# Graph attention on one core: gathers that leave out foreign edges, and 256-column fills on GpSimd

## The reference

```
q = (xn @ wq + bq).reshape(n, H, DH)            # H = 8 heads, DH = 32
k, v likewise; src, dst get one self edge for each node
scores = einsum('ehd,ehd->eh', q[dst], k[src]) * scale
ex = exp(scores - segment_max(scores, dst)[dst])
attn = ex / segment_sum(ex, dst)[dst]
agg = segment_sum(attn[:, :, None] * v[src], dst)
h = h + agg @ wo + bo ;  h = h + gelu(layernorm(h) @ w1 + b1) @ w2 + b2
```

## Time and profile before

| | us |
|---|---|
| median of 3 runs | 5238.9 (5233.25 to 5239.08) |
| profiled execution | 5237.06 |
| its span in the trace | 5235.3 |
| granted TensorE clock, mean | 0.899 of full speed |

### The profile page before, as it was taken

The page is one execution under the profiler, slowest core; times in us unless marked ns, Lnnn a source line. Parts: engine busy times, 40 slices in busy tenths (PEclk is TensorE's granted clock), DMA queues, the critical chain, the costliest instruction groups (busy, mean ns, idle before and its releaser), DMA issues. The chain is left out here.

```text
span 5235.3 us, 86953 instructions
## 1 busy us (share of the span) xinstructions
PE 3812.7 (73%) x17590; PEld 3000.8 (57%) x17591; DVE 3650.4 (70%) x9882; ACT 2132.3 (41%) x5069; POOL 3941.4 (75%) x4715
## 2 busy tenths in 40 slices
PE   1695777777777778888685777777777767777759
PEld 0344555555555567778443555555555557766646
DVE  3696888888888856666474888888888844444458
ACT  0113555555555523333113555555555523333322
POOL 2217888888888647777787888888888658888867
PEclk9898999999999989998896999899999978888879
DMA  3366666667666556666676766677666456666658
GB/s 112 118 201 199 201 199 199 197 197 201 198 196 199 144 129 140 139 130 134 117 156 176 203 197 199 197 196 202 199 198 197 134 128 127 125 123 126 132 142 238
DMA packets 664282, 882.62 MB, mean 169 GB/s; under 512 B 126257, under 2 KB 492269, under 8 KB 664013
## 3 DMA queue, kind: packets, MB, share of 16 engines
q0 software_dynamic: 261248, 529.64, 42.8%
q1 hardware_dynamic: 369907, 322.55, 20.8%
q10 hardware_dynamic: 32860, 28.05, 1.9%
HBM read 749.33 MB, written 130.59 MB: 168 GB/s over the span
## 5 line engine op out<-in xcount | busy, mean ns | idle before, releaser
L859 POOL DMA_INDIRECT kv<-kv_scratch,src_u x1760 | 1687.4, 959 | 364.3 <-POOL spacer L839 189.4
L1130 PE MATMUL sum_p<-msg,hot_s 128*128 128x273 f32 x3520 | 1091.6, 458 | 736.5 <-issue 499.5
L1318 POOL DMA_INDIRECT sum_scratch<-ysum,dest x700 | 1100.9, 1573 | 284.1 <-issue 153.5
L1130 PEld LDWEIGHTS sum_p<-msg,hot_s 128*128 128x128 f32 x3520 | 716.7, 215 | 1024.5 <-issue 697.5
L1118 PE MATMUL qe<-sums,hot_q 128*128 x3520 | 900.6, 401 | 74.5 <-ACT hot_q L890 48.8
L1118 PEld LDWEIGHTS qe<-sums,hot_q 128*128 128x128 f32 x3520 | 715.5, 206 | 216.9 <-issue 84.6
L996 DVE SCALAR_TENSOR_TENSOR sums<-sums,keep,sum_p 128x273 f32 x880 | 434.6, 494 | 436.7 <-PE sum_p L1130 326.5
L899 ACT ACTIVATE hot_s<-iota_f,ndrel_u 128x128 f32<-128x128 f32 x1760 | 559.4, 391 | 307.2 <-PE sum_p L1130 209.5
L970 DVE TENSOR_TENSOR prod<-qe,kv 128x1024 f32<-128x1024 f32 x440 | 535.9, 1218 | 67.5 <-DMA kv<-kv_scratch,src_u 66.4
L839 POOL MEMSET spacer<- 128x384 bf16 x1320 | 573.9, 435 | 0.9
L985 DVE TENSOR_TENSOR msg<-kv,turned 128x1024 f32<-128x1024 f32 x440 | 533.1, 1212 | 44.3 <-issue 34.6
(11 more groups left out here) (247 smaller groups left out, 5237.7 us busy)
## 6 DMA issues: line engine op xcount, KB each, us to landing
drow<-drel_scratch SPq DMA_DIRECT2D x220, 256.0 KB
ea<-in_edge_attr SPq DMA_DIRECT2D x100, 512.0 KB
srow<-in_src_rows SPq DMA_DIRECT2D x100, 512.0 KB
kv<-kv_scratch,src_u POOLq DMA_INDIRECT x1760
kv_scratch<-res SPq DMA_DIRECT2D x100, 256.0 KB
hin<-h_scratch SPq DMA_DIRECT2D x154, 128.0 KB
h_scratch<-res SPq DMA_DIRECT2D x150, 128.0 KB
masks<-mask_scratch SPq DMA_DIRECT2D x110, 128.2 KB
```

The source lines that it names most:

```text
L859: g.indirect_dma_start(out=kv[:, slot, :], out_offset=None, in_=KVd, in_offset=bass.IndirectOffsetOnAxis(ap=src_u[:, par, u:u + 1], axis=0 ...
L1130: ins = pe.matmul(sum_p[i][:, 0:XW], hot_s[:, q % 2, 2 * i + u, :], msg[:, q % 2, 2 * i + u, :], start=(u == 0), stop=(u == 1))
L1318: g.indirect_dma_start(out=sum_d[r], out_offset=bass.IndirectOffsetOnAxis(ap=dest[:, k, j:j + 1], axis=0), in_=ysum[:, k, j, :], in_offset ...
```

## The change

It has three parts. (1) The setup phase computes `later`, FAR = 8192 for units from number 48 on and else 0, and `skip`, which is `later` where an edge is not valid in its unit, and adds it to the source index. The first three periods (48 units) are left alone, so each ring slot is once filled in full. (2) The gather gets the bound NPA - 1 = 6911: an index above it is not fetched, and its row of `kv` keeps what it had. (3) The fills have 256 columns instead of 384.

```diff
+FAR = 1 << 13
+assert FAR >= NPA
...
+                    v.tensor_scalar(out=later[:, :], in0=unit_no[:, :], scalar1=float(RING * UB), scalar2=float(FAR),
+                                    op0=ALU.is_ge, op1=ALU.mult).then_inc(later_s, 1)
...
                     ins.then_inc(drel_done, 1)
-                    v.tensor_copy(srow_f[:, :, :], srow[:, :, :]).then_inc(srcf_done, 1)
                     v.wait_ge(drel_done, 1)
...
+                    v.wait_ge(later_s, 1)
+                    v.scalar_tensor_tensor(out=skip[:, :, :], in0=valid[:, :, :], scalar=0.0,
+                                           in1=later[:, :].unsqueeze(2).to_broadcast([P, IC, P]),
+                                           op0=ALU.is_equal, op1=ALU.mult).then_inc(skip_s, 1)
+                    v.wait_ge(skip_s, 1)
+                    v.scalar_tensor_tensor(out=srow_f[:, :, :], in0=srow[:, :, :], scalar=0.0, in1=skip[:, :, :],
+                                           op0=ALU.add, op1=ALU.add).then_inc(srcf_done, 1)
...
-                spacer = sb(ph, "spacer", [P, 3 * P], bf16)
+                spacer = sb(ph, "spacer", [P, 2 * P], bf16)
...
                                     g.indirect_dma_start(
                                         out=kv[:, slot, :], out_offset=None, in_=KVd,
-                                        in_offset=bass.IndirectOffsetOnAxis(ap=src_u[:, par, u:u + 1], axis=0)
-                                    ).then_inc(ring_in[par * GB + j], 16)
+                                        in_offset=bass.IndirectOffsetOnAxis(ap=src_u[:, par, u:u + 1], axis=0),
+                                        bounds_check=NPA - 1, oob_is_err=False).then_inc(ring_in[par * GB + j], 16)
```

More of the change, by code:

```diff
@@ L167, in gnn_kernel @@
             ge0 = sb(ph, "ge0", [P, IC, P])
+            skip = sb(ph, "skip", [P, IC, P])
+            later = sb(ph, "later", [P, IC])
             valid = sb(ph, "valid", [P, IC, P])
@@ L177, in gnn_kernel @@
             drel_done, key_done, srcf_done, tr_done, tr_out, stored, nt_stored, nt_in, dve_c, zeroed, z_out_s, grp, nt_zero = s.many(13)
-            drel_b_done = s.one()
+            drel_b_done, later_s, skip_s = s.many(3)
             with nc.Block() as block:
```

## The result

The changed kernel takes **5210.3 us** (median of 5, 5206.1 to 5215.6) against 5238.8: ratio **0.9945**, interval 0.9933 to 0.9956, so 28.5 us or 0.55% faster. Forecast were 5117 us. The time lies inside the stated range of 5045 to 5290, but the gain is a quarter of the forecast one; it is in the case "between the two", which had a chance of 0.13. The changed kernel's profiled span is 5208.5 us, 26.8 less than before.

What follows compares the result with a forecast made beforehand. GpSimd's instruction stream was taken to set the pace. 5237.1 - 144 (fills) + 2 (setup phase) + 20 (DVE catching up) = 5115 us for the profiled execution, 5117 us as median; range 5045 to 5290 us.

Steps and rivals of the forecast that it cites:

- between the two: Rival, chance 0.13: gathers 0.03 to 0.08 us dearer, or DVE and PE hold the period at 23.8 us; 5165 to 5228.
- The bound: Both attend stages: GpSimd's program text sets the pace, a period taking 24.46 us; fewer bytes alone are worth nothing.
- The fills: GpSimd's 1320 fills in the attend stages: each 109 ns shorter, 144 us in all, counted in full.
- The gathers' own time: 1760 GpSimd gathers: register move, comparison of 128 indices and rows left out each taken as 0 change from 959 ns.
- break-even: Extra cost per gather at which the change is worth nothing: 0.081 us, 8% of the gather's time.
- The page's rule: GpSimd cost per compared element: 0.11 to 0.22 us for a gather's 128 indices, making the sum 50 to 240 us slower.
- What is late next: DVE in attend: 20.9 us of work a period; catching up after long gaps at 16 turns charged with 20 us.
- Dearer gathers: Rival, chance 0.25: the bound's comparison costs over 0.081 us a gather; at 0.12 us, 5308 us.
- the main case: Chance 0.45: a gather takes what it took, within 0.025 us; 5117 us, 5070 to 5165.
- The signs named beforehand: Trace signs: gathers with 0.93 to 0.98 us mean if right; wrong if the mean is over 1.04 us.
- Cheaper gathers: Rival, chance 0.10: rows left out save gather time; by half of 0.10 us, to about 5026 us.
- the fills' time turning up as a gap: Rival, chance 0.07: no difference, the time saved on fills reappears as a gap ahead of each gather.

Runs made afterwards that it cites:

- all_far: The changed kernel with every index out of bounds from unit 48 on, so no k and v rows are fetched there: 5193.0 us, 0.9898 of the kernel before.
- bound_fill384: The kernel before with only the bound on each gather, all rows fetched, fills of 384 columns: 5332.0 us, 1.016.
- bound_reg: bound_fill384 with the bound in a register loaded once in each attend stage, not ahead of each gather: 5325.3 us, 1.0164 of the kernel before.
- fill256: The kernel before with only the fills narrowed to 256 columns, no bound, no rows left out: 5113.8 us, 0.975.
- no_fill: The kernel before without any fill and without the bound: 4809.2 us, 0.9176.
- skip_fill224: The changed kernel with fills of 224 columns: 5165.6 us, 0.9853 of the kernel before.

## Why the prediction was wrong

**The bound.** Right: GpSimd's row of instructions sets the pace of both attend stages. Every run with fills moved by what its GpSimd instructions moved, from 1.0173 to 0.9495, within some 15 us; transfers alone were worth at most the 15 us of all_far.

**The fills.** Right: 107 ns each for 109, 141 us for 144.

**The gathers' own time.** This is the step that failed: "The comparison of 128 indices: ... I take 0, nearest to that row." The bound costs 52 to 54 ns a gather, 95 us by the profile, 87 us by bound_fill384. The row that was taken as nearest compares two gathers of different row sizes; it says that a gather's time does not hang on bytes, and nothing on what happens to each index. What the compare itself costs was bounded only from afar, between 0 and 0.61 us. And the break-even worked out beside it, 0.081 us a gather, had shown that two thirds of that would eat most of the gain. (It leaves aside the 20 us that the sum charges for the catching up; with them it is 0.069.) The register move of 29 ns was rightly taken as hidden (bound_reg), and rows left out rightly as saving GpSimd nothing (all_far).

The page's rule (the Trainium skill, GPSIMD Engine Reference, "Performance pitfalls for Q7 kernels": a cost for each element of a compare-and-select) had the sign right. The estimate from it was 0.11 to 0.22 us; the measured 0.054 us is half of the lower end. By it the change would have been slower; by the measurement it is faster. Whether the 0.054 us go to compares at all is open, since no run has another number of indices.

**What is late next.** Charged with 20 us for DVE's catching up; fill256 lost 10 of its 141. DVE's work of 20.9 us a period was right, as no_fill shows. What was missing is the meeting of the copy and the rescaling. It was to be seen ahead: the copy at 1414.62 took 0.40 us, the one at 1420.83 0.29, and the rescaling stood at 1414.47. So the kernel before paid for it already, and the parts alone show more than their own effect: fill256 has 5 us less of copies than before (128.5 for 133.6), bound_fill384 6 us less (127.2), while the whole change has 5.5 us more (139.1). That is 17 us between parts and whole. Against it stand 6 us of gaps ahead of gathers, which fill256 has and the whole change has not, and with it go the 2 us of the setup phase, which no part has: 13 of the 15 us. That copies and rescaling hinder each other is shown by where each copy ends, and by the table of widths; that this is all of the 15 us is an account of the rows, not shown by the times.

**The sum.** With the measured 95 us in place of 0 for the bound, the prediction's own sum gives 5212 us, and 5210.3 were measured. That it comes so near is in part luck: the 20 us charged for catching up were some 10, and the meeting, charged with nothing, filled their place.

**The rivals.** Dearer gathers came true as a mechanism, below the point from which it decides; "a gather is 0.03 to 0.08 us dearer" is what happened, with 5165 to 5228 us. (Its upper end does not follow from its price: 0.08 us over 1760 gathers on top of 5117 would be 5258; and the dearer case's 5308 leaves out the 20 us of catching up that the main case has.) The signs named beforehand had a hole: 0.93 to 0.98 us stood for right and over 1.04 for wrong, and 1.013 came. Cheaper gathers have fallen (all_far), and so has the fills' time turning up as a gap (fill256).

## What to carry to other kernels

Where one engine's instructions follow each other without holes, nearly every nanosecond in its loop is paid in full, and work spared on another resource is worth next to nothing: here 50 MB less of traffic cost 87 us to ask for. An option of an instruction that the trace doesn't show is best given its break-even per instruction first; if that is under a tenth of the instruction's time, a forecast of "free" is a guess. And before a filler is made shorter to pay for something, it should be tried alone, and taken out altogether: here that alone was worth 8%.

## What the runs showed of the hardware

A bound on an indirect DMA of 128 rows costs GpSimd 52 ns in the median (956 and 1008 ns), whether no row (bound_fill384), 11% (the changed kernel) or nearly all (all_far) are out of bounds. A row out of bounds keeps its place in a packet and moves 4 bytes of its 2048 (261,248 packets with 529.64, 480.06 and 94.28 MB). In all_far a gather lands after 2.1 us in the median, a full one in no_fill after 3.9. GpSimd's fill of bf16 takes 0.84 ns a column (221, 301, 328, 355 and 435 ns for 128, 224, 256, 288 and 384). A GpSimd copy that starts in the first 0.2 us of the rescaling, a DVE operation with two SBUF inputs, ends 0.13 to 0.14 us after the rescaling does (0.17 at most), and so takes up to 0.26 us longer (0.55 for 0.29 us, all_far). In skip_fill224 11 copies that started 0.030 to 0.035 us ahead of the rescaling were held as well (0.58 to 0.61 us), while 39 that started 0.036 to 0.051 us ahead kept 0.29 us. A gather that meets it takes up to 0.28 us longer (1.29 for 1.01 us, all_far).
